# Ten of sixteen expert-output tiles added up inside the second attention's first turns, two tiles a turn, with paired inverse roots

## What is computed

```python
x = x + tanh(g_xattn[0]) * L0_xattn(ctx, _layernorm(x), ...)
x = x + tanh(g_ffn[0]) * L0_ffn(_layernorm(x), ...)          # 16 experts + a shared one
x = x + tanh(g_xattn[1]) * L1_xattn(_layernorm(x), ctx, ctx, ...)   # 16 heads of width 8
x = x + tanh(g_ffn[1]) * L1_ffn(_layernorm(x), ...)          # ternary weights, rounded rows
```

## Time and profile before

| what | us |
|---|---|
| times of three runs | 415.06, 418.20, 418.32 |
| their median | 418.2 |
| the profiled execution, its own time | 416.1 |
| its span, first to last instruction | 414.3 |
| PE busy in the span | 379.6 (92%) |
| DVE busy | 331.3 (80%) |
| ACT busy | 260.9 (63%) |
| POOL busy | 226.3 (55%) |

### The profile page before, as it was taken

One profiled execution on the slowest core, in us unless ns is written; L12 is line 12 of the kernel. 1 busy time (PEld: TensorE's weight loads), 2 busy tenths in 40 slices (PEclk: granted clock), 3 DMA queues, 4 the chain that ended last, 5 costly groups with the idle time before them and its releaser, 6 DMA issues. The chain is left out here.

```text
span 414.3 us, 10614 instructions
## 1 busy us (share of the span) xinstructions
PE 379.6 (92%) x3648; PEld 279.5 (67%) x3662; DVE 331.3 (80%) x925; ACT 260.9 (63%) x514; POOL 226.3 (55%) x372
## 2 busy tenths in 40 slices
PE   7799999999999999999999999998888887887885
PEld 7356766666666666677658888685766766676664
DVE  4789999899989999887555886555568888887996
ACT  2478767777777777667652222444577676767964
POOL 4475587666676666635040000378288887867630
PEclk9999999999999999999999999999999999999999
DMA  5979999700000000000000000000000000000012
GB/s 147 259 147 120 125 129 131 68 2 2 2 2 2 1 2 2 2 2 3 0 2 2 0 0 2 2 0 2 2 2 2 3 2 2 2 2 2 2 40 65
DMA packets 61284, 13.29 MB, mean 32 GB/s; under 512 B 51488, under 2 KB 60592, under 8 KB 61232
## 3 DMA queue, kind: packets, MB, share of 16 engines
q1 hardware_dynamic: 59776, 11.94, 21.5%
q10 hardware_dynamic: 1328, 0.66, 0.5%
q0 software_dynamic: 128, 0.00, 0.0%
HBM read 11.55 MB, written 1.05 MB: 30 GB/s over the span
## 5 line engine op out<-in xcount | busy, mean ns | idle before, releaser
L397 POOL TENSOR_TENSOR a_rn<-a_ssq,neghalf 128x8 f32<-128x8 f32 x48 | 79.0, 1655 | 30.1 <-DVE a_ssq L996 25.5
L996 DVE TENSOR_REDUCE a_ssq<-q_home 128x8 f32<-128x512 f32 x48 | 32.3, 672 | 6.5 <-ACT q_home L783 6.5
L91 POOL TENSOR_TENSOR moments<-moments,eps_row 128x1 f32<-128x1 f32 x32 | 6.2, 195 | 54.9 <-DVE moments L86 54.6
L486 PE MATMUL a_x<-wkv_a,a_kvT 128*128 128x512 f32 x64 | 34.5, 621 | 0.9 <-ACT kv_home L789 0.8
L789 ACT ACTIVATE kv_home<-a_x,maskcol 128x512 f32<-128x512 f32 x32 | 21.9, 685 | 18.4 <-PE a_x L486 18.4
L1854 DVE TENSOR_REDUCE b_mx<-b_s 128x16 f32<-128x1024 f32 x16 | 19.6, 1224 | 10.3 <-PE b_s L1490 10.2
L1344 POOL TENSOR_TENSOR b_k<-b_ksb,quad 128x256 f32<-128x256 f32 x32 | 19.0, 614 | 14.1 <-ACT b_ksb L1698 14.1
L413 POOL TENSOR_TENSOR a_yr<-a_ymv,eps_row 128x1 f32<-128x1 f32 x16 | 3.1, 192 | 38.0 <-DVE a_ymv L1039 38.0
L1015 DVE TENSOR_REDUCE a_mx<-a_s 128x4 f32<-128x512 f32 x32 | 21.9, 686 | 2.0 <-PE a_s L512 1.9
L801 ACT ACTIVATE kv_home<-a_m,cols 128x512 f32<-128x512 f32 x32 | 22.0, 687 | 0.8 <-PE a_m L500 0.7
L531 PE MATMUL a_m<-kv_home,p_home 128*64 128x65 f32 x512 | 22.0, 228 | 0.3 <-ACT p_home L811 0.3
(11 more groups left out here) (294 smaller groups left out, 1169.3 us busy)
## 6 DMA issues: line engine op xcount, KB each, us to landing
w_gu<-in_L_ffn_Wg_dram SPq DMA_DIRECT2D x4, 512.0 KB, 9.3
w_gu<-in_L_ffn_Wu_dram SPq DMA_DIRECT2D x4, 512.0 KB, 11.0
w_d<-in_L_ffn_Wd_dram SPq DMA_DIRECT2D x8, 256.0 KB, 8.0
out_dram<-xs SPq DMA_DIRECT2D x8, 128.0 KB, 1.9
xs<-in_x_dram SPq DMA_DIRECT2D x1, 640.0 KB, 11.6
cs<-in_ctx_dram SPq DMA_DIRECT2D x1, 640.0 KB, 11.4
wkv_a<-in_L_xattn_Wkv_dram SPq DMA_DIRECT2D x1, 512.0 KB, 7.6
nat<-in_L_ffn_w_dram SPq DMA_DIRECT2D x2, 256.0 KB, 3.1
```

The lines of the kernel that those rows point to most:

```text
L397: nc.gpsimd.tensor_tensor(rn[:, tp, i, :], ssq[:, tp, i, :], neghalf[:, 0:H0], ALU.pow)\
L486: nc.tensor.matmul(p_x[:], kvT[:, tp, b * 2 * S:(b + 1) * 2 * S], wkv_a[:, INNER:2 * INNER], start=True, stop=True).then_inc(vproj_done, 1)
L996: nc.vector.tensor_reduce(ssq[:, tp, i, :], sq[:, i, :].rearrange("p (h d) -> p h d", h=H0), AX.X, ALU.add).then_inc(reduced, 1)
```

## The change

The first loop handles only the first six tiles (`FIRST = 6`). Tiles 6 to 15 are handled by pairs in the second loop, by the table `TWO` = {1: 6, 2: 8, 3: 10, 4: 12, 5: 14}: in PE's turns 2 to 6. There PE waits for `shifted` of the last scores right after the projection, transposes both tiles of the pair into banks 0 and 1, and after the transposed attention adds up both into banks 2 and 3; `scores` of that turn also waits for the pair's `x_summed`. ACT copies both out before `exp`; DVE adds both and takes both tiles' statistics before `row_max`, and their moments after it. POOL takes both roots at once (`inverse_roots`, 2 columns) after the spread keys of its turns 5 to 9. The pieces of the attention in the first loop move to earlier tiles, the ternary weights are turned between the scores of tile 0 and turn 2, and the fill matmuls of `BUSY` are gone.

```diff
+    def inverse_roots(pool, t):
+
+        var = moments[:, 1, t:t + 2, 1]
+        pool.wait_ge(mv_ready, t + 2)
+        nc.gpsimd.tensor_tensor(var, var, eps_row[:, 1:2].to_broadcast([P, 2]), ALU.add).then_inc(var_ready, 2)
+        pool.wait_ge(var_ready, t + 2)
+        return nc.gpsimd.tensor_tensor(var, var, neghalf[:, 0:2], ALU.pow)
...
-    BUSY = {1: 2, 2: 2, 3: 1}
+
+
+    FIRST = 6
+    TWO = {i + 1: t for i, t in enumerate(range(FIRST, NT, 2))}
...
-            for t in range(NT):
+            for t in range(FIRST):
                 sum_root(pool, t).then_inc(rooted, 1)
-                if t in (0, 1, 6):
+                if t < 2:
                     pool.wait_ge(rooted, t + 1)
-                    normalise(min(t, 2), t % 2)
-                if t == 10:
+                    normalise(t, t)
+                if t == 3:
+                    normalise(2, 0)
                     spread_keys(0, 0)
             pool.wait_ge(ready, 1)
-            pool.wait_ge(rooted, NT)
...
+                if s - 4 in TWO:
+                    sum_roots(pool, TWO[s - 4]).then_inc(rooted, 2)
...
                 if exists(s, NT):
+                    pool.wait_ge(rooted, max(s + 1, FIRST))
                     normalise(s, s % 2)
...
             def scores(t, tp):
                 wait(pe, shifted, t)
-                busy(nc, p_s[:, 0, 0:256], ident[:], v["wq_a"][:, 0:256], BUSY.get(t, 0))
+                if t == 0:
+                    pe.wait_ge(turn_ready, FIRST)
+                    pe.wait_ge(x_summed, FIRST)
+                if t in TWO:
+                    pe.wait_ge(x_summed, TWO[t] + 2)
...
-            for s in range(NT + 1):
-                if exists(s, NT):
+            for s in range(FIRST + 1):
+                if s < FIRST:
                     turn_outputs(s, s % 2)
-                if exists(s - 1, NT):
+                if s >= 1:
                     add_up(s - 1, (s - 1) % 2)
-                if s in (2, 4):
-                    turn_context(s // 2 - 1)
-                if s in (6, 9):
-                    turn_input(s // 3 - 2, s // 3 - 2)
-                if s == 8:
+                if s in (1, 2):
+                    turn_context(s - 1)
+                if s in (4, 6):
+                    turn_input(s // 2 - 2, s // 2 - 2)
+                if s == 5:
                     project(0, 0)
-                if s in (10, 12):
-                    turn_ternary(s // 2 - 5)
-            pe.wait_ge(x_summed, NT)
-            pe.wait_ge(turn_ready, NT)
...
                 if s >= 2 and exists(s - 1, NT):
                     project(s - 1, (s - 1) % 2)
+                if s - 1 in TWO:
+                    pe.wait_ge(shifted, s - 1)
+                    turn_outputs(TWO[s - 1], 0)
+                    turn_outputs(TWO[s - 1] + 1, 1)
                 if exists(s - 3, NT):
                     mix(s - 3, (s - 3) % 2, 1)
...
                     turn_attention(s - 3, (s - 3) % 2)
+                if s - 1 in TWO:
+                    add_up(TWO[s - 1], 0)
+                    add_up(TWO[s - 1] + 1, 1)
                 if exists(s - 1, NT):
                     scores(s - 1, (s - 1) % 2)
+                if s == 1:
+                    turn_ternary(0)
+                    turn_ternary(1)
...
                 if exists(s - 1, NT):
                     projections_out(s - 1, (s - 1) % 2)
+                if s - 1 in TWO:
+                    outputs_out(TWO[s - 1], 0)
+                    outputs_out(TWO[s - 1] + 1, 1)
...
                     hidden(s - 5)
+                if s in TWO:
+                    for i in range(2):
+                        add_outputs(TWO[s] + i, i)
+                    for i in range(2):
+                        sum_stats(dve, TWO[s] + i, i, x_summed)
                 if exists(s, NT):
                     row_max(s, s % 2)
+                if s in TWO:
+                    for i in range(2):
+                        sum_moments(dve, TWO[s] + i, i)
```

More of the change, by code:

```diff
@@ L93, in inverse_root @@
         return nc.gpsimd.tensor_tensor(var, var, neghalf[:, 0:1], ALU.pow)
-    return row_stats, row_moments, inverse_root
+    def inverse_roots(pool, t):
[4 more added lines that the diff above has]
+        return nc.gpsimd.tensor_tensor(var, var, neghalf[:, 0:2], ALU.pow)
+    return row_stats, row_moments, inverse_root, inverse_roots
 def build(nc, x, ctx, mask, g_xattn, g_ffn, ln_x_w, ln_x_b, ln_l_w, ln_l_b, Wq, Wkv, q_scale, k_scale, Wo,
@@ L257, in first_half @@
         proj_bank, p_m, p_s = (p_q, p_y, p_k), (p_m0, p_m1), (p_s0, p_s1)
-        row_stats, row_moments, inverse_root = next_norm(nc, v, ph, "a0")
+        row_stats, row_moments, inverse_root, _ = next_norm(nc, v, ph, "a0")
         first_in, second_in, third_in, wq_in, wkv_in, wo_in, affine_in, scale_in, small_in, mask_in = (
@@ L1323, in attention_ffn @@
             sem(n) for n in ("turn_done", "turn_ready", "sum_done", "x_summed", "rooted"))
-        sum_stats, sum_moments, sum_root = next_norm(nc, v, ph, "c")
+        sum_stats, sum_moments, sum_root, sum_roots = next_norm(nc, v, ph, "c")
         @block.sync
@@ L1749, in ternary_out @@
                 nc.scalar.copy(w, p_y[:]).then_inc(tern_out, 1)
-            for t in range(NT):
+            for t in range(FIRST):
                 outputs_out(t, t % 2)
-                if t in (2, 4):
-                    context_out(t // 2 - 1, t // 2 - 1)
-                if t in (6, 9):
-                    input_out(t // 3 - 2, t // 3 - 2)
-                if t == 8:
-                    act.wait_ge(zeroed, 3)
-                    projections_out(0, 0)
-                if t == 10:
-                    ternary_out(0, w1_t[:])
-                if t == 12:
-                    ternary_out(1, w2_t[:].rearrange("p c k -> p (c k)"))
+                if t in (1, 2):
+                    context_out(t - 1, t - 1)
+                if t == 4:
+                    input_out(0, 0)
+            act.wait_ge(zeroed, 3)
+            projections_out(0, 0)
+            input_out(1, 1)
+            ternary_out(0, w1_t[:])
+            ternary_out(1, w2_t[:].rearrange("p c k -> p (c k)"))
             for s in range(2, NT + 1):
@@ L1828, in add_outputs @@
                                                ALU.mult, ALU.add).then_inc(x_summed, 1)
-            for s in range(NT + 2):
-                if exists(s - 2, NT):
+            for s in range(FIRST + 2):
+                if exists(s - 2, FIRST):
                     sum_moments(dve, s - 2, s % 2)
-                if exists(s, NT):
+                if exists(s, FIRST):
                     add_outputs(s, s % 2)
-                if exists(s - 1, NT):
+                if exists(s - 1, FIRST):
                     sum_stats(dve, s - 1, (s - 1) % 2, x_summed)
```

## The result

The changed kernel takes 422.9 us (median of six, 420.82 to 425.91); the kernel before, with three more executions, 416.83 (415.06 to 418.85). The ratio is 1.0148, 95% interval 1.0108 to 1.0188: **slower by about 1.5%**. The profiled execution is one of the typical ones, 422.97 us.

The account below looks back on a forecast made before the run. The prediction took the ring of attention, scores, projection and POOL's keys as the bound. Terms -11.75, +13.4 and +0.8 gave +2.45: 418.55 us on the profiled 416.1, 419.3 on the 416.9 mean; range 415 to 424.

Parts of the forecast that it names:

- The ring of projection, keys and attention: Second loop, turns 4 to 6: transposed attention, scores, projection, POOL's keys, attention again bound the kernel; 6.00 us a lap.
- The start: First loop up to tile 0's scores: ended by POOL's keys, at 273.1 instead of 284.85, 11.75 us gained.
- the rivals: The one meant: tile 0's keys come later, POOL held up by DVE's ternary steps; 420.5 at +2 us; chance 0.04.
- Lap 1: From tile 0's scores to tile 1's: 7.15 us at full clock, against 4.64 before.
- the prediction's own sign: Granted clock after 270 us: a dip there would show the forecast wrong.
- The price of the fall: PE's work on the first lap's path doubled at 1.2 GHz: scores 0.65, transposes 0.33, add-ups 1.65, together +2.6 us.
- Laps 2 to 5: Second-loop laps with a pair: 8.45, 8.8, 9.17 and 9.35 us, against 6.71, 6.32, 5.88 and 6.00 before.
- The last pair's roots: POOL's paired roots in a short lap delay DVE's normalised rows, subtraction and second mix: 0.8 us lost, bounds 0 and 1.05.
- The sum: Whole kernel: -11.75 at the start, +13.4 in five laps, +0.8 for the final paired roots, giving +2.45 us.
- the rival with the clock: TensorE falls to 1.2 GHz in the thin stretch before tile 0's scores: +4 us more, 422.5, slower by 1.5%; chance 0.20.
- within 1%: Whole kernel's time differs from the kernel before by less than 1% (4.2 us); chance 0.65.

Follow-up runs that it names:

- both edits: Changed kernel plus six fill matmuls ahead of tile 0's scores and POOL's paired roots moved behind the ffn's rows; ratio 1.0114 to the kernel before.
- the last two versions: Eight first-loop tiles, transposes behind mix, roots behind ffn's rows, three fill matmuls; one also has probabilities transposed before scores, moments after subtraction (0.9955), the other not (0.9946).

## Why the prediction was right or wrong

- **What bounds the kernel.** Right as far as the laps show it. The ring of projection, keys and attention ran the laps that have no pair, and the laps with one were ended by the attention and the add-ups behind it.
- **The start.** Right in what ends it, POOL's keys, and right in size by luck: 273.1 forecast, 273.30 measured, with two errors that cancel. POOL came to the third normalise at 270.32 and not at 271.07 (0.34 of this because its first root already came earlier, at 264.88 against 265.22), and then took longer than I had priced (rows of the changed kernel's trace):

```profile
270.32 1.13 POOL L1348 TENSOR_SCALAR b_xn<-xs,moments 128x128 f32<-128x128 f32 x1
...
270.56 0.75 DVE L1871 TENSOR_SCALAR b_tern<-b_tern 128x1024 f32<-128x1024 f32 x1
...
271.42 1.63 POOL L1355 TENSOR_TENSOR b_k<-b_ksb,quad 128x256 f32<-128x256 f32 x2
271.50 1.08 DVE L1874 TENSOR_SCALAR b_tern<-b_tern 128x1024 f32<-128x1024 f32 x1
```


The third normalise takes 1.13 and the keys 1.63, where 0.80 and 1.20 were taken from the earlier trace rows: together 0.76 more, which puts the end of the keys at 273.05 against 273.07. The step of 0.25 from there to the scores I had not priced. DVE's ternary step beside the keys takes 1.08, and 0.68 in the kernel before; the one beside the normalise takes 0.75. The Trainium skill's page "SBUF — State Buffer" (Who interferes with whom) says that a `tensor_scalar` in a 2-port mode and GpSimd contend for one port pair and that the later one waits for the other's end. The rows agree that there is contention, but not that one side is blocked in full: the normalise, which starts first, is stretched by 0.33 and DVE's step by 0.07, then the keys by 0.43 and DVE's step by 0.40, and either pair ends sooner than the two would one after the other. No run here separates the two engines. I had named this among the rivals and priced the forecast without it.

- **Lap 1.** The term that failed. 7.15 was forecast and 7.29 measured at full clock (in the run with fill matmuls), but 9.59 in the changed kernel: 2.30 of it is the clock at 1.2 GHz. The stretch was named and its length was right (270.5 to 273.1 against 270.3 to 273.3); the step that failed is the choice to leave the fall out of the sum with a chance of 0.20. What I had set against it, shows only stretches with more work. By the prediction's own sign, a granted clock that dips after 270, the forecast is wrong here. The price of the fall, 2.6, was near the 2.30, but not for the reason given: 1.65 of it were the add-ups, which ran at full clock (the scatter at 280.94 takes 0.44). What the half clock stretched is what stands ahead of them, from the scores and the ternary transposes to the projection and the pair's transposes: counted from the scores, the first of these pair transposes starts 5.68 behind them and 3.51 with fill. The page "TensorE: Matmul & The Clock Gate" (Part 1: The HAM clock gate) of the Trainium skill, by which the half clock is the state of rest, had spoken for the fall; the trace agrees, with 1.00 to 0.50 behind the idle stretch.
- **Laps 2 to 5.** Right: 35.8 forecast, 36.3 measured; the late subtraction and the pushed mix are there, and moving the transposes behind the mix took 3.1 off. That the copies of ACT are free there fits the laps too.
- **The last pair's roots.** Right in place and size, 0.8 forecast and 0.99 measured in lap 7. What followed was not foreseen: the clock fell again behind the wait that it makes on PE, 1.14 in lap 8. It did so in two of the four profiles that have this wait.
- **The sum.** +2.45 forecast; +6.9 in the profiled span, of which about 3.4 is the clock (2.3 and 1.1). The rest, 3.5, and the 3.2 of the run with both edits are the change at full clock, near the 2.45 forecast. The time of 422.9 lies in the range and next to the 422.5 given for the rival with the clock, in part by luck: its 4 us allowed for a fall that lasts into lap 2, which it did not do, and the second fall was not in it. By the chances, "within 1%" at 0.65 was the wrong first choice; the ratio's interval, 1.0108 to 1.0188, is slower by over 1%, for which 0.28 was given.
- **Why deferring a pair gains so little here.** From the first transpose to tile 0's scores it is 23.48 with sixteen tiles in the first loop and 12.87 with eight: 1.33 a tile, 2.66 a pair. In a lap a pair costs about 2.4 (8.25 to 8.31 against 5.88), even when its transposes are hidden, since the two add-ups and the round trip of 0.89 through DVE stand there in full. So a pair gains some 0.3 as long as the first loop itself sets the start, down to eight tiles. The next pair takes only 0.5 more off the start (12.38), because POOL's keys are then the end of it, and loses about 2.

## What to carry to other kernels

Work that is moved into the gaps of a loop brings its own round trip with it; compare that with the part of it that is really hidden, and stop moving where another engine becomes the end of the stretch that is being shortened. Two blocks that both fit into a wait should stand so that the one somebody else waits for comes first: here the order of mix and transposes was worth 3.1 us of 7. And a stretch in which PE has nothing should be priced with the work behind it at half the clock too, not only as an idle stretch.

## What the runs showed of the hardware

- The fall is not tied to the idle time alone. 3.0 us idle ahead of tile 0's scores brought one in every profile that had no fill there (three of three), and none with fill (the two versions with six tiles that have it); 1.0 us, with eight tiles in the first loop, brought one in one of three; 1.46 us in the lap of the last pair's roots brought one in two of four; 2.73 us in the kernel before without fill brought one in its only profile. Its price is not fixed either: with the same 3.0 us, lap 1 is 9.59, 9.60 and 8.67 against 7.29.
- The clock falls in places that none of the edits touch. Of the kernel before, beside the last two versions, executions with a mean clock of 0.987 or 0.988 took 418.3 to 420.1 us and those at 0.995 to 1.000 took 415.0 to 416.5, but for two at 0.996 with 417.6 and 418.1. Two profiles of other versions (both edits, and the transposed probabilities ahead of the scores) show where such a loss can sit: a fall from about 199 to 206 us, where PE is busy all the time (4.00 of 4.00), which costs about 3.5 us. Three profiles (both edits, eight tiles, the kernel before without fill) have a short fall between 378 and 392, behind idle stretches of 0.5 and 0.8 that the kernel before and the changed one have too, without a fall; it costs next to nothing. No run here was aimed at its cause, and whether it is what the kernel before loses in some executions stays open, since its profile has no fall. For a change of 1% this spread is as large as the effect, and the laps in the profiles tell more than the medians do.
